# A chunked Mamba-style scan on one core: the gated y turned by the DMA crossbar, and the upper bound filled in banks of its own

## What is computed

```python
xr, gate = jnp.split(x @ W_in.T, 2, axis=-1)
xr = xr + t_emb[:, None, :]
xc = silu(causal_conv4(xr) + b_conv)
xn = layernorm(xc) * ln_g + ln_b
Bm, Cm, dt = jnp.split(xn @ W_xproj.T, 3, axis=-1)
Ad = 1.0 + 0.01 * tanh(dt @ W_dt.T + b_dt) * (-tanh(A_log))
Bd = Bm * minimum(norm(xn), 1.0)
def step(h, inputs):
    h = jnp.clip(h * ad[:, :, None] + bd[:, :, None] * xt[:, None, :], -10.0, 10.0)
    return h, jnp.einsum('bd,bdh->bh', ct, h)
y = scan(step) + D * xn
out = x + y * silu(gate) @ W_out.T
```

## Time and profile before

| | before |
|---|---|
| median of 3 runs | 2083.74 us (2082.17 to 2084.46) |
| profiled execution, its own time | 2086.27 us |
| its span | 2084.4 us |
| mean granted TensorE clock | 0.985 of full speed |
| busy: PE, POOL, DVE, ACT | 92%, 84%, 77%, 66% |
| DMA, mean | 59 GB/s |

### The profile page before, as it was taken

One profiled execution on the slowest core, in us unless ns is written; L12 is line 12 of the kernel. 1 busy time (PEld: TensorE's weight loads), 2 busy tenths in 40 slices (PEclk: granted clock), 3 DMA queues, 4 the chain that ended last, 5 costly groups with the idle time before them and its releaser, 6 DMA issues.

```text
span 2084.4 us, 46452 instructions
## 1 busy us (share of the span) xinstructions
PE 1916.6 (92%) x16624; PEld 1441.5 (69%) x16624; DVE 1603.2 (77%) x2045; ACT 1377.9 (66%) x3462; POOL 1747.5 (84%) x1444
## 2 busy tenths in 40 slices
PE   5589999999999999999999999999999999999988
PEld 5467776776776776776677777676777677777665
DVE  3377887878887877887787887787887787887786
ACT  4577666677666667766676766776766676766643
POOL 1388888889888889888889988889988888988886
PEclk9699999999999999999999999999999999999999
DMA  5121212121212121212121112221112121121110
GB/s 175 57 63 44 63 48 63 56 68 44 62 47 63 56 68 49 58 47 63 56 68 52 56 46 64 58 65 53 56 48 64 56 64 57 53 58 53 55 54 16
DMA packets 98437, 122.37 MB, mean 59 GB/s; under 512 B 31072, under 2 KB 68336, under 8 KB 93536
## 3 DMA queue, kind: packets, MB, share of 16 engines
q1 hardware_dynamic: 98208, 119.41, 20.1%
HBM read 62.07 MB, written 9.31 MB: 34 GB/s over the span
## 4 chain that ended last, share of the span: by engine, by line
PE 50%; ACT 18%; issue 15%; DVE 12%; POOL 2%; SPq 2%; DMA 1%; DVEq 0%; ACTq 0%; POOLq 0%
PE ps_y L588 10%; DVE ks L981 7%; PE ps_job L465 7%; PE ps_job L503 7%; PE ps_fill L561 6%; PE ps_fill L552 5%; PE ps_job L478 4%; ACT low L786 4%; ACT tap L744 3%; PE ps_y L568 3%; PE ps_job L472 2%; ACT xh L682 2%; ACT lend L764 1%; ACT gate L676 1%; DVE pf L932 1%
## 5 line engine op out<-in xcount | busy, mean ns | idle before, releaser
L1079 POOL TENSOR_TENSOR prod<-ks,crep 128x512 f32<-128x512 f32 x1024 | 1286.7, 1276 | 159.0 <-DVE ks L981 153.4
L981 DVE TENSOR_TENSOR_SCAN ks<-low,ps_fill 128x512 f32<-128x512 f32 x1024 | 1208.1, 1208 | 255.4 <-PE ps_fill L561 251.6
L786 ACT COPY low<-ps_fill 128x512 f32<-128x512 f32 x1024 | 585.1, 581 | 534.3 <-PE ps_fill L552 534.2
L588 PE MATMUL ps_y<-c_sb,prod 128*128 128x128 f32 x4096 | 610.9, 274 | 2.2 <-POOL prod L1079 1.4
L588 PEld LDWEIGHTS ps_y<-c_sb,prod 128*128 128x128 f32 x4096 | 459.3, 142 | 80.2 <-issue 43.4
L561 PE MATMUL ps_fill<-spans,pick 128*128 128x512 f16 x1024 | 390.3, 381 | 61.8 <-ACT low L786 51.8
L552 PEld LDWEIGHTS ps_fill<-ts,xs 128*128 128x128 f16 x4096 | 315.2, 98 | 174.5 <-issue 8.5
L552 PE MATMUL ps_fill<-ts,xs 128*128 128x128 f16 x4096 | 397.4, 220 | 11.8 <-DVE ks L981 6.0
L744 ACT ACTIVATE tap<-xr,cols_sb 128x128 f32<-128x128 f32 x768 | 251.7, 392 | 0.0
L460 PE MATMUL ps_job<-x,w_in 128*128 128x128 f16 x3072 | 216.5, 222 | 10.3 <-POOL x L1049 7.8
L465 PE MATMUL ps_job<-w_in,x 128*128 128x512 f16 x768 | 203.2, 381 | 21.3 <-ACT gate L676 21.3
(11 more groups left out here) (123 smaller groups left out, 2063.8 us busy)
## 6 DMA issues: line engine op xcount, KB each, us to landing
crep<-c_dram SPq DMA_DIRECT2D x32, 1024.0 KB, 4.8
xs<-xh SPq DMA_DIRECT2D x256, 64.0 KB, 2.0
xs<-xl SPq DMA_DIRECT2D x224, 64.0 KB, 2.0
xf<-in_xT SPq DMA_DIRECT2D x32, 256.0 KB, 2.8
res<-in_x SPq DMA_DIRECT2D x32, 256.0 KB, 2.6
out_dram<-res SPq DMA_DIRECT2D x32, 256.0 KB, 2.1
ts<-tth SPq DMA_DIRECT2D x128, 32.0 KB
ts<-tth SPq DMA_DIRECT2D x128, 31.0 KB
```

Source lines behind the costliest of these rows:

```text
L588: last = mm(ps_y[:, cut], prod[:, (TILES * k + s) % HOLD, e, :], ident, start=False, stop=(u % 4 == 3 and q == 3 and e == QN - 1), is_tran ...
L786: copy(low[:, (TILES * k + s) % RING], ps_fill[:, (TILES * k + s) % RING]).then_inc(sem["low_copied"], 1)
L981: nc.vector.tensor_tensor_scan(ks[:, u % 2, QN * q:QN * (q + 1)].rearrange("d n t -> d (n t)"), low[:, g % RING], ps_fill[:, g % RING], 0. ...
L1079: tt(prod[:, g % HOLD], ks[:, u % 2, part], crep[:, p, part], ALU.mult).then_inc(sem["weighed"], 1)
```

## The change

It does two things. First, the gated y is no longer transposed by PE. DVE writes the gated half into a bank of `ps_job`, ACT and DVE split it into fp16 halves `y16` in the layout that it has, and SP issues two transposing DMAs for each half chunk (`turn`) into `yT`. One `turn` stands between the copies of `xh` and those of `xl`, the other after the transfers of h and ahead of the output's store. The job `out` starts two points later, and waits for the DMAs. ACT's first gate of a chunk waits for the DMAs of the half whose `y16` lies in `gate`.

Second, `widen`, `pick` and `spans` are gone. `ts` gets a second copy for the upper bound, which differs in the two bound rows alone; `fill` is called twice for a tile, for the lower bound in two banks (three tiles ahead) and for the upper one in three banks (two tiles ahead). SP sends each of the twelve pieces of `ts` once for each copy, and the bounds in four transfers each way in place of three.

```diff
-RING = 5
-AHEAD = 3
+LOWS = 2
+HIGHS = 3
+LOWRING = 4
+AHEAD = (3, 2)
...
-        ts = sb("ts", [P, 2, NSUB, NS * SUB], H)
+        ts = sb("ts", [P, 2, 2, NSUB, NS * SUB], H)
...
-                (8, 4, "gate", 1, 0, 2, 0), (10, 1, "yT", 1, -1, 2, 1),
+                (7, 1, "yT", 1, -1, 2, 1), (8, 4, "gate", 1, 0, 2, 0),
...
-                (41, 12, "out", 0, -1, 1, 1), (46, 9, "conv", 1, 2, 2, 0), (54, 1, "yT", 0, 0, 2, 1),
+                (39, 1, "yT", 0, 0, 2, 1), (43, 12, "out", 0, -1, 1, 1), (46, 9, "conv", 1, 2, 2, 0),
...
-        N_STACK = 16 * (3 * NSUB + NSUB - 1)
-        N_BOUND = 16 * 3
+        N_STACK = 16 * (6 * NSUB + NSUB - 1)
+        N_BOUND = 16 * 4
...
+            def turn(j, i):
+                sp.wait_ge(sem["yT_taken"], 2 * j + i + 1)
+                since(sp, "out_ready", j)
+                for a in range(2):
+                    sp.dma_start(yT[:, a, 4 * i:4 * i + 4, :], y16[i][:, a], transpose=True
+                                 ).then_inc(sem[f"yT_in{i}"], 16)
...
                     sp.dma_start(x0[:], x0_dram.broadcast_to([NS, DI])).then_inc(sem["x0_in"], 16)
+                if exists(k, -1):
+                    turn(k - 1, 1)
+                if exists(k, 1):
                     sp.wait_ge(sem["xl_done"], j + 1)
...
                     sp.wait_ge(sem["tt_done"], 2 * (j + 1))
-                    for jj in range(NSUB):
-                        a = SUB * jj
-                        for r, half in ((0, tth), (SUB, ttl), (2 * SUB, tth)):
-                            lead = 0 if r == 2 * SUB else 1
-                            sp.dma_start(ts[r + lead:r + SUB, pn, jj],
+                    for v in range(2):
+                        for jj in range(NSUB):
+                            a = SUB * jj
+                            for r, half in ((0, tth), (SUB, ttl), (2 * SUB, tth)):
+                                lead = 0 if r == 2 * SUB else 1
+                                sp.dma_start(ts[r + lead:r + SUB, pn, v, jj],
...
+                if exists(k, 0):
+                    turn(k, 0)
                 if exists(k, -1):
...
-                since(pe, "scanned", g - RING + 1)
+                if v == 0:
+                    since(pe, "low_copied", g - LOWS + 1)
+                else:
+                    since(pe, "scanned", g - HIGHS + 1)
...
-            def widen(k, p, s):
-                q = s % NQ
-                pe.wait_ge(sem["low_copied"], TILES * k + s + 1)
-                mm(ps_fill[:, (TILES * k + s) % RING], pick[:], spans[:, p, q * BANK:(q + 1) * BANK], start=False, stop=True,
...
+                    ahead(k, p, s + AHEAD[0], 0)
+                    ahead(k, p, s + AHEAD[1], 1)
...
-                    since(act, "yT_ready", 2 * (k - 1) + i + 1)
+                    if i == 0:
+                        since(act, "yT_in0", N_YT * k)
+                    else:
+                        since(act, "y_gated", 2 * k)
...
-                tt(gate[:, half], ps_y[:], gate[:, half], ALU.mult).then_inc(sem["y_gated"], 1)
+                bank_free(dve, k + i, [job[2:4] for job in JOBS].index(("yT", i)))
+                tt(bank("yT", i), ps_y[:], gate[:, half], ALU.mult).then_inc(sem["y_gated"], 1)
...
-                    dve.wait_ge(sem["bounded"], g + 1)
+                    dve.wait_ge(sem["low_copied"], g + 1)
+                    dve.wait_ge(sem["high_filled"], g + 1)
```

More of the change, by code:

```diff
@@ L170, in build @@
         xs = sb("xs", [P, 2, NSUB, DI], H)
[L171 to L174 removed]
+        ts = sb("ts", [P, 2, 2, NSUB, NS * SUB], H)
+        low = sb("low", [P, LOWRING, BANK])
         ks = sb("ks", [P, 2, NS, P])
@@ L299, in later_loads @@
                     carry = A["carry"].rearrange("r (j c) -> r j c", j=NSUB)
-                    loads.append((ts[96:128, p], carry))
+                    for v in range(2):
+                        loads.append((ts[96:128, p, v], carry))
                 for dst, src in loads:
@@ L362, in body @@
                     sp.wait_ge(sem["bound_all"], j + 1)
[L363 to L367, removed]
+                    for v, bound in enumerate((scratch, r_dram)):
+                        for h in range(2):
+                            sp.dma_start(bound[h].rearrange("j n t -> n j t"),
+                                         bnd16[:, h, v].rearrange("n (j t) -> n j t", j=NSUB)
+                                         ).then_inc(sem["bound_out"], 16)
                     sp.wait_ge(sem["c_out"], 16 * (j + 1))
@@ L375, in body @@
                                      ).then_inc(sem[f"ones_in{pn}"], 16)
[L376 to L383, removed]
[L384 to L391 removed]
+                    sp.wait_ge(sem["bound_out"], 64 * (j + 1))
+                    for v, bound in enumerate((scratch, r_dram)):
+                        for h in range(2):
+                            sp.dma_start(ts[SUB * h:SUB * h + 1, pn, v].rearrange("o j c -> o (j c)"),
+                                         bound[h].rearrange("(o j) n t -> o (j n t)", o=1)
+                                         ).then_inc(sem[f"bound_in{pn}"], 16)
+                    sp.wait_ge(sem["tt_done"], 2 * (j + 1))
+                    for v in range(2):
+                        for jj in range(NSUB):
[3 more added lines that the diff above has]
+                                sp.dma_start(ts[r + lead:r + SUB, pn, v, jj],
+                                             half[a + lead:a + SUB].rearrange("s n t -> s (n t)")).then_inc(stack, 16)
                     sp.wait_ge(sem["lend_set"], 2 * j + 2)
@@ L440, in job @@
                 _, parts, name, i, off, per, bank = JOBS[m]
-                if not exists(k, off):
+                if not exists(k, off) or name == "yT":
                     return
@@ L493, in job @@
                     last = mm(ps[:, 0:2], spread, bd[:], start=True, stop=True)
[L494 to L497, removed]
                 elif name == "out":
@@ L535, in inputs, with fill @@
                         pe.wait_ge(sem["w_low"], len(pieces))
-                    pe.wait_ge(sem["yT_taken"], 2 * j + 1)
-            def fill(k, p, s):
+                    pe.wait_ge(sem["yT_in0"], N_YT * (j + 1))
+            def fill(k, p, s, v):
                 g = TILES * k + s
                 u, q = divmod(s, NQ)
-                if s == 0:
+                if s == 0 and v == 0:
                     if isinstance(k, int) and k == 0:
@@ L620, in body, with ahead @@
                     jobs_at(k, p, 2 * s + 1)
+            def ahead(k, p, s, v):
+                if s < TILES and exists(k, 0):
+                    fill(k, p, s, v)
+                elif s >= TILES and exists(k, 1):
+                    fill(k + 1, 1 - p, s - TILES, v)
             steps(body)
@@ L668, in side @@
                         continue
-                    take("yT", i, -i, 2)
-                    copy(yT[:, 0, 4 * i:4 * i + 4, :],
-                         bank("yT", i).rearrange("d (e t) -> d e t", e=4)).then_inc(sem["yT_high"], 1)
+                    act.wait_ge(sem["y_gated"], 2 * (k - i) + i + 1)
+                    if i == 1:
+                        since(act, "yT_in1", N_YT * (k - 1))
+                    copy(y16[i][:, 0], bank("yT", i)).then_inc(sem["yT_high"], 1)
                 for i in at("gate", 0):
                     take("gate", i, 0, 2)
-                    since(act, "yT_ready", 2 * (k - 1) + i + 1)
+                    if i == 0:
+                        since(act, "yT_in0", N_YT * k)
+                    else:
+                        since(act, "y_gated", 2 * k)
                     act_fn(gate[:, i * BANK:(i + 1) * BANK], bank("gate", i), ACT.Silu, scale=1 / WS
@@ L719, in side @@
                     since(act, "bound_all", k + 1)
-                    since(act, "bound_out", 48 * (k + 1))
-                    for v, clip in enumerate((-CLIP, 2 * CLIP)):
+                    since(act, "bound_out", 64 * (k + 1))
+                    for v, clip in enumerate((-CLIP, CLIP)):
                         act_fn(ad[:, v], pf[:, 0], ACT.Identity, scale=clip).then_inc(sem["bound32"], 1)
@@ L784, in copy_low @@
                 def copy_low(k, s):
-                    act.wait_ge(sem["filled"], TILES * k + s + 1)
-                    copy(low[:, (TILES * k + s) % RING], ps_fill[:, (TILES * k + s) % RING]).then_inc(sem["low_copied"], 1)
+                    act.wait_ge(sem["low_filled"], TILES * k + s + 1)
+                    since(act, "scanned", TILES * k + s + 1 - LOWRING)
+                    copy(low[:, (TILES * k + s) % LOWRING], ps_fill[:, (TILES * k + s) % LOWS]).then_inc(sem["low_copied"], 1)
                 for s in range(TILES):
[L789 to L792, removed]
+                    if s + AHEAD[0] < TILES and exists(k, 0):
+                        copy_low(k, s + AHEAD[0])
+                    elif s + AHEAD[0] >= TILES and exists(k, 1):
+                        copy_low(k + 1, s + AHEAD[0] - TILES)
                     side(k, p, 2 * s)
```

62 lines of the change are left out of this document (25 added, 37 removed).

## The result

| | before | after |
|---|---|---|
| median | 2083.74 us | 2393.98 us (2392.49 to 2395.87, 4 runs) |
| ratio to before, 95% interval | | 1.149 (1.1471 to 1.151) |
| profiled execution, its span | 2086.27, 2084.4 us | 2393.44, 2391.6 us |
| mean granted TensorE clock | 0.985 | 0.918 |

What follows compares the result with a forecast made beforehand. PE, 92% busy, looked the bound, but the DMA chain behind `ttl` would set the step: 45.1 + 27.8 = 72.9 us. 31 x 10.8 plus 12 at the start, added to 2086.3, gives 2433 us; range 2300 to 2510.

Steps and rivals of the forecast that it cites:

- The loop and its price: First fill to first fill: PE waits for h every step, 72.9 us, 10.8 more than 62.15; chance 0.65.
- From `ttl` to the fill: From POOL's end of `ttl` through SP's queue and DMA to PE's first fill: 15.83 + 12.0 = 27.8 us.
- The term of twelve pieces: Twelve more pieces of `ts` on SP's queue between `ttl` and h: 12.0 us, bounds 8.23 and 12.1.
- From the fill to `ttl`: From PE's first fill to POOL's next end of `ttl`: 45.55 less 0.43, 45.1 us; bounds 43.0 and 47.7.
- The transposing DMAs at nothing: Both pairs per step on SP's queue cost nothing, covered by SP's idle 4.6 us and 12 us before ACT's gate.
- The transposes as a gain of 27.5 us if PE sets the step: Taking 64 transposing jobs of y, 0.43 us each, off PE gains 27.5 us, 0.86 per step, if PE bounds.
- Widen for a fill at nothing: On PE, a second fill in place of each widen costs nothing, within 0.01 us a tile, 10 us in all.
- the wait for ACT's copy stays: In the tile loop, widen's wait for ACT's copy, 51.8 us in all, stays at the lower fill.
- The faster case: PE sets the step and the DMA is hidden: 27.5 us gained from transposes, 2058 us; chance 0.05.
- the slack: Before PE's first fill, time the DMA chain has to spare: 17.84 us left, 15.83 needed, 2.0 us per step.
- SP's pace alone: Pieces of `ts` do not pile up below SP: twelve cost 8.2 us, step 69.1, time 2311 us; chance 0.17.
- The slow transposes: Transposing DMAs of some 10 us or more hold ACT's gate and PE; at 12 us each 2588 us; chance 0.11.

Runs made afterwards that it cites:

- the run with `tth` early: Changed kernel with SP sending the 16 pieces of `tth` once that half is there and the 8 of `ttl` after; 2324.67 us, ratio 1.1155.
- the fills alone: Changed kernel with PE's transposes of y back and no transposing DMA; 2400.12 us, ratio 1.1514.
- the pieces hidden: Changed kernel with y transposed by PE, 32-row pieces, both copies in one DMA, `tth` early, bounds last; 2083.52 us, ratio 0.9996.
- the run with twelve pieces: Changed kernel without the second copy of `ts`, the upper fill reading the lower bound's operands (output not the reference's); 2049.93 us, ratio 0.9831.
- the run with rows of 32: Changed kernel with all 24 pieces of `ts` sent as 32 rows and the bounds sent after they landed; 2272.74 us, ratio 1.0899.
- twelve double ones: Changed kernel with both copies of a `ts` piece in one transfer, twelve issues, still 31, 31 and 32 rows; 2415.59 us, ratio 1.1593.

## Why the prediction was right

**The loop and its price.** The forecast was that every step waits for h, with 72.9 us a step and 2433 us in all. PE's longest wait is that one, 306.9 us against the 310 named; the step is 71.7. Per step that is 9.5 us more than before, 31 x 9.5 = 295, and the span grew by 307.2. The rest, some 12 us, is at the start, as forecast: the first fill of all begins at 100.40 us in place of 87.21. The 39 us by which 2433 is too high are 31 times the 1.25 us of the step that follow.

**From `ttl` to the fill**, 27.8 forecast, 27.1 measured. The term of twelve pieces was 12.0 and measured 27.1 - 15.83 = 11.3. Counted on the queue, 24 pieces and the pile behind them make 19.7 + 4.0 = 23.7, less the 12.1 of the first twelve: 11.6. The sum held, its picture did not: I had the second twelve pile up behind SP ("24 pieces in some 16.5 us", "`lend` landing about 10 us after its issue"). SP took 19.7, and `lend` landed in 6.0. The pile did not grow; SP was held. For the fill it is the same, since h stands behind both. One reading was too narrow as well: the 6% of the earlier trace rows are those of one microsecond. Over the six behind it the share is 0.15, since pieces of 32 rows are under way too, and only the 0.07 of the run with `tth` early, where 31 rows go out alone, shows one engine at work:

```profile
1012.00:1018.00 6.00, 6.00 (x48) 4.19 (x47) 3.38 (x4) 3.83 (x12) 4.12 (x4) 1.00 0.15 41
```

**From the fill to `ttl`**, 45.1 forecast, 44.6 measured. I carried over the 2.6 us that the one stalled step of before had lost. POOL's scale came 4.13 us after the fill, not 3.32, but the stretch behind it lost less, 40.5 against 39.64. The low clock after the wait came as expected.

**The transposing DMAs at nothing**: right. 128 KB land in 2.6 us and a pair takes SP some 2.6. The first pair took up most of SP's idle time ahead of `xl`: of 141.7 us in 31 waits, 21.8 in 23 are left. In the other eight steps SP came to `xl` when it was done, but no wait of PE for the copies of `xl` shows. ACT's first gate did not wait for the transposing DMAs. The Trainium skill's "Advanced Engine Details and Errata" (X-Bar Transpose), by which they are as fast as other DMAs, is near the measurement: 2.6 us against 2.0 for a copy of half the size. The estimate of 5.2 us, worked out from the Trainium skill's "VectorE: DVE Perf Modes" (The three transpose paths), is twice the measured 2.6; the measurement decides.

**The transposes as a gain of 27.5 us if PE sets the step**: mis-sized. From start to start one moved PE on by 0.43 us, but a job was worth 40.6 / 64 = 0.63 beside the new fills, with PE as the bound, and 21.5 / 64 = 0.34 beside the old ones. It made no difference to the forecast, where PE's own time vanished in its wait, as it did: 6 us between the fills alone and the whole change.

**Widen for a fill at nothing**: right for the time, 0.9996 of before with the pieces hidden. PE's busy time grew by 14.0 us and its rest shrank by 16.8. That the wait for ACT's copy stays was wrong. It fell from 51.8 us to 7.0 in the changed kernel, and a wait of the fills for DVE's scan, 6.0 us before, took its place:

```profile
PE ps_fill L567 <- DVE ks L994: 76.0, 94, 8.8
...
PE ps_fill L567 <- ACT low L799: 7.0, 30, 0.2
```

Beside the wait for h it did not count.

**The rivals.** The faster case needed the second twelve pieces to cost no more than the slack; the run with twelve pieces has that, and gives 2049.93 where 2058 was priced. SP's pace alone, priced at 2311, is nearest to the run with rows of 32: no pile, and 2272.74. That price kept the 3.9 us that the first twelve leave below SP, which are gone there too, and had no bounds behind h. The slow transposes fall with the 2.6 us. The upper end of the range is 2516 by its own sum, 2086 + 430, not 2510.

## What to carry to other kernels

Before you add transfers to a queue, find the transfer behind them that the bounding engine waits for, and measure its slack in one step; here 2 us of slack stood against some 11 of new work, in a kernel whose PE read 92% busy. Then look at what each transfer needs below the queue, not at its issue alone: one row less in a piece made 24 pieces cost 23.7 us in place of 16, and fewer issues did not help. Try a change of two parts with one part hidden or fixed as well: the same transposes were worth 21.5, 40.6 or 6 us, according to what set the step beside them.

## What was not expected of the hardware

SP's issues are held once some 4 to 5 us of transfers lie below it: `lend`, which takes 2.4 us with nothing piled up, landed in 5.9 to 6.1 us behind twelve pieces, 24, or twelve double ones, and in 7.1 where the last eight pieces all had 31 rows, while single issues grew from about 0.6 us to 1.1 and up to 3.2. A backlog of DMA therefore shows as long issues, and the landing times alone do not tell its size.
